# Four weights of a fused graph network rounded by ScalarE with their low parts on GpSimd, and two row splits moved behind the first group's last scaling

## The reference

```python
def reference(x, adj, nodemask, ...):
    x = _layernorm(x + _L0_gnn_ref(x, nodemask, adj, adj, W_qkv, W_out, b_out))   # attention
    x = _layernorm(x + _L1_gnn_ref(x, adj, W))                                    # mean aggregation
    x = _layernorm(x + _L2_gnn_ref(x, adj, W1, b1, gamma, beta, W2, b2))          # hypergraph
    x = _layernorm(x + _L3_gnn_ref(x, adj, Wqk, bqk, Wl, bl, Wr, Wd, bd))         # gated similarity
    return x

# L0: 8 heads of 64: attn = 0.33 * softmax(q k^T / 8, masked) + 0.33 * adj + 0.33 * exp(-adj)
#     out = (attn v) @ W_out + b_out
# L1: relu([x, (adj x) / max(deg, eps)] @ W^T)
# L2: h = relu(G (x W1^T) + b1); h = layer_norm(h) * gamma + beta; y = G (h W2^T) + b2; y + x
#     G = D^-1 H B^-1 H^T, H = (adj != 0), D weighted with adj's first row
# L3: xg = x * sigmoid(deg * Wd + bd); QK = sigmoid(xg Wqk^T + bqk); S = QK QK^T / 16 * adj
#     relu((S / rowsum) xg Wl^T + bl + xg Wr^T)
```

## Time and profile before

| | us |
|---|---|
| three timed runs, median (lowest, highest) | 1227.41 (1226.9, 1227.48) |
| the profiled execution, its time | 1225.61 |
| its span, first to last instruction | 1223.7 |
| TensorE busy (share of the span) | 1168.5 (95%) |
| VectorE busy | 896.1 (73%) |
| ScalarE busy | 586.5 (48%) |
| GpSimd busy | 583.7 (48%) |
| TensorE's granted clock, mean share of full speed | 0.981 |

### The profile page before, as it was taken

The page is one execution under the profiler, slowest core; times in us unless marked ns, Lnnn a source line. Parts: engine busy times, 40 slices in busy tenths (PEclk is TensorE's granted clock), DMA queues, the critical chain, the costliest instruction groups (busy, mean ns, idle before and its releaser), DMA issues.

```text
span 1223.7 us, 30667 instructions
## 1 busy us (share of the span) xinstructions
PE 1168.5 (95%) x11472; PEld 1037.0 (85%) x11472; DVE 896.1 (73%) x1983; ACT 586.5 (48%) x1186; POOL 583.7 (48%) x747
## 2 busy tenths in 40 slices
PE   5789999999999999999999999999999999999866
PEld 4678898988989898898989889898988989898755
DVE  3775777777777777777777777777777777778753
ACT  3336454454545445454544545454454545445231
POOL 2416447272644727264472726447272644727150
PEclk9799999999999999999999999999999999999897
DMA  7000002010010201001020100102010010100000
GB/s 221 23 27 23 23 2 66 2 45 21 15 49 0 64 0 43 21 14 51 0 64 0 43 21 13 51 0 64 0 43 21 12 52 0 47 2 27 1 22 18
DMA packets 52726, 37.12 MB, mean 30 GB/s; under 512 B 28166, under 2 KB 47564, under 8 KB 52684
## 3 DMA queue, kind: packets, MB, share of 16 engines
q1 hardware_dynamic: 51816, 36.14, 9.8%
q10 hardware_dynamic: 868, 0.40, 0.2%
HBM read 28.14 MB, written 8.39 MB: 30 GB/s over the span
## 4 chain that ended last, share of the span: by engine, by line
PE 91%; DVE 4%; POOL 2%; ACT 1%; issue 1%; DMA 1%; POOLq 0%; SPq 0%; DVEq 0%
PE bank L981 21%; PE bank L983 20%; PE bank L982 20%; PE bank L1177 7%; PE bank L1085 3%; PE bank L1052 3%; PE bank L1121 2%; PE bank L1063 2%; PE bank L1246 2%; PE bank L1229 2%; PE bank L1042 1%; PE bank L1150 1%; PE bank L1093 1%; PE bank L1219 1%; PE bank L1166 1%
## 5 line engine op out<-in xcount | busy, mean ns | idle before, releaser
L462 POOL TENSOR_SCALAR var<-mv 128x2 f32<-128x2 f32 x128 | 29.2, 228 | 381.3 <-DVE mv L764 381.2
L588 ACT ACTIVATE v<-bank 64x256 f32<-64x256 f32 x256 | 96.8, 378 | 77.5 <-PE bank L983 74.8
L771 DVE TENSOR_SCALAR x<-x,mv,rstd 128x256 f32<-128x256 f32 x256 | 120.2, 516 | 12.0 <-POOL rstd L465 12.0
L760 DVE BATCH_NORM_STATS2 stats<-x 128x6 f32<-128x256 f32 x256 | 96.4, 419 | 4.4
L465 POOL TENSOR_TENSOR rstd<-var,negh 128x2 f32<-128x2 f32 x128 | 91.0, 711 | 10.7
L887 DVE TENSOR_TENSOR hT_lo<-r,hT_hi 128x512 fp32r<-128x512 f32 x64 | 68.7, 1108 | 33.8 <-ACT hT_hi L616 33.8
L534 POOL TENSOR_TENSOR prob<-prob,mix 128x512 f32<-128x512 f32 x64 | 87.8, 1373 | 6.0 <-POOL prob L529 1.9
L529 POOL TENSOR_TENSOR prob<-prob,srec 128x512 f32<-128x512 f32 x64 | 70.8, 1107 | 40.0 <-DVE srec L812 40.0
L576 ACT ACTIVATE pT<-bank 128x512 f32<-128x512 f32 x64 | 34.5, 589 | 98.7 <-PE bank L1063 98.7
L694 DVE TENSOR_TENSOR spT_lo<-bank,spT_hi 128x512 fp32r<-128x512 f32 x64 | 44.2, 691 | 51.1 <-ACT spT_hi L576 51.1
L981 PE MATMUL bank<-wo_hi,oT_hi 128*128 128x256 f32 x256 | 76.0, 297 | 3.6 <-DVE oT_lo L694 3.4
(11 more groups left out here) (213 smaller groups left out, 3908.4 us busy)
## 6 DMA issues: line engine op xcount, KB each, us to landing
xTin<-in_x_t SPq DMA_DIRECT2D x32, 256.0 KB, 2.9
xin<-in_x SPq DMA_DIRECT2D x16, 512.0 KB, 3.7
out_x<-x SPq DMA_DIRECT2D x32, 256.0 KB, 2.2
adjA<-in_adj SPq DMA_DIRECT2D x16, 128.0 KB, 2.6
adjB<-in_adj SPq DMA_DIRECT2D x32, 64.0 KB, 3.2
adjC<-in_adj SPq DMA_DIRECT2D x32, 64.0 KB, 2.3
r<-in_wqkv SPq DMA_DIRECT2D x2, 512.0 KB, 8.5
x<-in_wqkv SPq DMA_DIRECT2D x1, 512.0 KB, 10.5
```

The costliest lines, as they stand in the source:

```text
L588: ins = act.activation(v[e * N:(e + 1) * N, i, gr, :, :], src[gr * N:(gr + 1) * N, e], ACT.Copy)
L760: dve.bn_stats(stats[layer][:, t, :], src[:, t, :]).then_inc(SEM[f"stats{n}"], 1)
L771: ins = dve.tensor_scalar(x[:, t, :], x[:, t, :], mv[layer][:, t, 0:1], rstd[layer][:, t:t + 1], ALU.subtract, ALU.mult)
```

## The change

Four of the five weights of group 0 (w1, wm, wqk and W2) are no longer split by VectorE. ScalarE rounds w1, wm and wqk behind its step `pv` 0 and W2 behind its `pv` 3; each counts the new semaphore `rounded`. GpSimd subtracts: the low parts of w1, wm and wqk behind its `soft` 3, that of W2 behind the reciprocal root of `norm0` 1; each counts `others_ready`. VectorE's `other_weights(0)` keeps only the two scalings of W2, `other_weights(1)` goes away, `other_weights(2)` keeps `tbc`, the correction and the two extra columns. The six instructions on adjacency's first row and the six on the bias row move to the end of `other_weights(3)`. Waits follow: VectorE's `norm0` 0 waits for w1's low part (its buffer is overwritten), ScalarE's `graph_a` for three low parts, TensorE's `mean` for two and `up` for four.

```diff
@@ -272,6 +272,9 @@
         w2_scaled = ctx.enter_context(nc.semaphore("w2_scaled"))
         ones_ready = ctx.enter_context(nc.semaphore("ones_ready"))
         weights_ready = ctx.enter_context(nc.semaphore("weights_ready"))
+        rounded = ctx.enter_context(nc.semaphore("weights_rounded"))
+        w2_fixed = ctx.enter_context(nc.semaphore("w2_fixed"))
+        others_ready = ctx.enter_context(nc.semaphore("other_weights_ready"))
         early_in = ctx.enter_context(nc.semaphore("early_in"))
         zero_ready = ctx.enter_context(nc.semaphore("zero_ready"))
         parted = ctx.enter_context(nc.semaphore("parted"))
@@ -489,6 +492,13 @@
                     pool.wait_ge(*count("sqsum", g, i - 1))
                 pool.tensor_tensor(r[:, 0, :], r[:, 0, :], r[:, i, :], ALU.add).then_inc(SEM["sqsum"], 1)
 
+            def norm0(g, i):
+                inv_root(g, 0, "0", 2 * i, 2 * i + 2, i)
+                if isinstance(g, int) and g == 0 and i == 1:
+                    pool.wait_ge(rounded, 4)
+                    pool.tensor_tensor(w2[1][:, :, 0:D], raw_2, w2[0][:, :, 0:D].bitcast(F32),
+                                       ALU.subtract).then_inc(others_ready, 1)
+
             def mean_h(g, i):
 
                 pool.wait_ge(*count("msq_ready", g, 1))
@@ -533,10 +543,15 @@
                 t = k - k % 2
                 pool.tensor_tensor(u, u, mix[:, t:t + 2, :].rearrange("p t (a n) -> p t a n", a=1)
                                    .broadcast_to([P, 2, HP, N]), ALU.add).then_inc(SEM["attn_ready"], 1)
+                if isinstance(g, int) and g == 0 and k == T - 1:
+                    for n, (pair, src) in enumerate(((w1, raw_1), (wm, raw_m), (wqk, raw_qk))):
+                        pool.wait_ge(rounded, n + 1)
+                        pool.tensor_tensor(pair[1][:, :, :], src, pair[0][:, :, :].bitcast(F32),
+                                           ALU.subtract).then_inc(others_ready, 1)
 
             steps = {
                 "soft": soft, "mask": residual,
-                "norm0": lambda g, i: inv_root(g, 0, "0", 2 * i, 2 * i + 2, i),
+                "norm0": norm0,
                 "graph_a": graph_a, "graph_b": graph_b, "gate": gate_argument, "split_low": split_low,
                 "mean": lambda g, i: inv_root(g, 1, "1", 2 * i, 2 * i + 2, i),
                 "hyper": lambda g, i: inv_root(g, 2, "2", 2 * i, 2 * i + 2, i),
@@ -598,9 +613,18 @@
                 src = bank_of("oT", i)
                 ins = act.activation(oT[0][:, i % 2:HP:2, :], src[:, :].rearrange("p (a n) -> p a n", a=HP // 2), ACT.Copy)
                 ins.then_inc(SEM["oT_hi"], 1)
+                if isinstance(g, int) and g == 0 and i == 0:
+                    act.wait_ge(weights_in, 16 * 8)
+                    for pair, src in ((w1, raw_1), (wm, raw_m), (wqk, raw_qk)):
+                        act.activation(pair[0][:, :, :], src, ACT.Copy).then_inc(rounded, 1)
+                if isinstance(g, int) and g == 0 and i == T - 1:
+                    act.wait_ge(w2_fixed, 1)
+                    act.activation(w2[0][:, :, 0:D], raw_2, ACT.Copy).then_inc(rounded, 1)
 
             def graph_a(g, i):
                 act.wait_ge(*filled("ht", 0, g))
+                if isinstance(g, int) and g == 0:
+                    act.wait_ge(others_ready, 3)
                 src = bank_of("ht", 0)
                 act.activation(flat(hTb[:, :, :]), src[:, 0:T * P // 2].bitcast(BF16), ACT.Copy)
                 ins = act.activation(flat(hT0[:, :, :]), src[:, 0:T * P // 2].bitcast(BF16), ACT.Copy)
@@ -712,7 +736,6 @@
 
                 if i == 0:
                     dve.wait_ge(weights_in, 16 * 8)
-                    split_weight(w1, raw_1)
                     dve.wait_ge(bias_in, 16 * 8)
                     for c in range(HC):
                         dve.tensor_scalar(xl[2][:, c, :], raw_2[:, c, :], bet[:, c:c + 1], None,
@@ -722,16 +745,7 @@
                     for c in range(HC):
                         dve.tensor_scalar(raw_2[:, c, :], raw_2[:, c, :], gam[:, c:c + 1], None,
                                           ALU.mult).then_inc(w2_scaled, 1)
-                    dve.wait_ge(zero_ready, 6)
-                    bias_parts(b2row, 0, 2 * D)
-                if i == 1:
-                    split_weight(wm, raw_m)
-                    split_weight(wqk, raw_qk)
                 if i == 2:
-
-                    three_parts([row0p[:, :, k] for k in range(3)], row0, gmat[:, 0, 0:T * GRP],
-                                gT[:, 0, 0:T * GRP])
-
                     dve.wait_ge(t_full, 1)
                     dve.tensor_copy(tbc[:, :], bank[7][:, 0:D]).then_inc(setup_dve, 1)
                     done[0] += 1
@@ -741,17 +755,21 @@
                     ones = one[:, :].rearrange("p (a k) -> p a k", a=1).broadcast_to([P, HC, 2])
                     setup(dve.tensor_copy(w2[0][:, :, D:D + 2], ones))
                     setup(dve.tensor_tensor(w2[1][:, :, D:D + 2], ones, ones, ALU.subtract))
-                    split_weight([half[:, :, 0:D] for half in w2], raw_2)
+                    dve.sem_inc(w2_fixed, 1)
                 if i == 3:
 
                     setup(dve.tensor_scalar(raw_lr, raw_lr, 0.5, None, ALU.mult))
                     setup(dve.tensor_scalar(bqk[:, :], bqk[:, :], 0.5, None, ALU.mult))
                     split_weight(wlr, raw_lr)
+                    three_parts([row0p[:, :, k] for k in range(3)], row0, gT[:, 0, 0:T * GRP],
+                                gT[:, 0, T * GRP:2 * T * GRP])
+                    dve.wait_ge(zero_ready, 6)
+                    bias_parts(b2row, 0, 2 * D)
 
             def pv(g, i):
                 low_part(g, "oT", i, oT[1][:, i % 2:HP:2, :], oT[0][:, i % 2:HP:2, :], "oT")
-                if isinstance(g, int) and g == 0 and i < 2:
-                    other_weights(i)
+                if isinstance(g, int) and g == 0 and i == 0:
+                    other_weights(0)
 
             def norm(g, layer, src, lo, hi):
 
@@ -816,6 +834,8 @@
                 dve.wait_ge(*filled("out0", i, g))
                 src = bank_of("out0", i)
                 dve.wait_ge(*count("xb_ready", g, 1))
+                if isinstance(g, int) and g == 0 and i == 0:
+                    dve.wait_ge(others_ready, 1)
                 ins = dve.tensor_tensor(flat(xl[0][:, lo:hi, :]), src[:, :], flat(xin[:, lo:hi, :]), ALU.add)
                 ins.then_inc(SEM["sum0_ready"], 1)
                 dve.wait_ge(*count("sum0_ready", g, i + 1))
@@ -1184,7 +1204,7 @@
 
             def mean(g, i):
                 if isinstance(g, int) and g == 0 and i == 0:
-                    pe.wait_ge(weights_ready, 6)
+                    pe.wait_ge(others_ready, 2)
                 pe.wait_ge(*count("turn1_lo", g, 2))
                 pe.wait_ge(*emptied("mean", i, g))
                 two_tiles("mean", i, lambda t: [(tile_of(x1T, c, t), chunk(wm, c)) for c in range(C)]
@@ -1198,7 +1218,8 @@
             def up(g, i):
                 if isinstance(g, int) and g == 0 and i == 0:
 
-                    pe.wait_ge(weights_ready, 9)
+                    pe.wait_ge(others_ready, 4)
+                    pe.wait_ge(weights_ready, 5)
                 pe.wait_ge(*emptied("up", i, g))
                 dst = bank_of("up", i)
                 now_full(product(dst[:, :], [(chunk(w1, c, slice(i * P, (i + 1) * P)), chunk(spT, c)) for c in range(C)],
```

## The result

The changed kernel takes 1233.74 us, median of 4 runs (1233.39 to 1235.09), the kernel before 1227.16 beside it (4 runs, 1224.25 to 1227.48). The ratio is 1.0061, 95% interval 1.0044 to 1.0078: slower by 0.4 to 0.8%. The profiled execution took 1235.09, with a span of 1233.3; it is the longest of the four.

What follows compares the result with a forecast made beforehand. TensorE, busy 95% of the span, was taken as the bound; +3.7 - 4.5 + 6.9 + 1.0 = +7.1 us on the profiled 1225.6 gave 1232.7, and the median's 1.8 more made 1234.5. The range was 1227.5 to 1238.

Steps and rivals of the forecast that it cites:

- `w2_sums` starts later: TensorE's start of `w2_sums`, held by VectorE's W2 scalings waiting on GpSimd's instructions: +3.7 us.
- `w2_sums` itself: Length of `w2_sums` on TensorE, left at 4.77 us, half at the low clock; bounds 3.14 and 6.40.
- second gap closes: TensorE's 3.43 us wait before `out0` 1 goes and it runs at full clock: -4.5 us, bounds -3.1 and -4.9.
- idle time before `graph_a`: TensorE waits for VectorE's longer chain to `edge`: 7.2 less 0.33 makes +6.9 us, bounds 4.4 and 7.2.
- low clock around `agg`: Low TensorE clock behind the new idle time before `graph_a`: +1.0 us, between 0 and 1.9.
- One scaling a turn: VectorE's eight W2 scalings pass singly between GpSimd's instructions, the last three after wqk, ending near 55.4 us.
- The rival of one run: VectorE and GpSimd, 45 to 49 us: all eight scalings pass together before 48.7; total -1.3, 1226.1 us; chance 0.13.
- the rival of two a turn: Two scalings pass between GpSimd instructions, the eighth ending near 52.2 us; `w2_sums` +0.6, total +4.0, 1231.4; chance 0.15.
- first rival: Not slower: VectorE's eight scalings pass in one run, `w2_sums` follows without a gap; 1226.1 us; chance 0.13.
- third rival: Low clock lasts longer: all of `w2_sums` low, +1.6, and +0.9 before `agg`; total +9.6, 1237.0 us; chance 0.15.
- the 0.33 in hand: Slack between VectorE finishing `edge` at 79.65 and TensorE taking it up at 79.98: 0.33 us.
- fourth rival: W2's low part on GpSimd does not delay `scale0` 1's scalings: -2.5, so total +4.6, 1232.0 us; chance 0.07.

Runs made afterwards that it cites:

- The filled gap: The changed kernel with 24 matmuls, their result overwritten, ahead of TensorE's wait for the scalings before `w2_sums`: 1233.65 us, ratio 1.0057 to the kernel before.
- the run with W2's low part later: The changed kernel with W2's subtraction on GpSimd moved from behind `norm0` 1 to behind `graph_b` of group 0: 1230.38 us, ratio 1.0034 to the kernel before.
- the subtractions that wait: The changed kernel with GpSimd's three subtractions behind `soft` 3 waiting until the eight W2 scalings are done: 1225.98 us, ratio 0.9998 to the kernel before.
- the second with filler: Repeat of the changed kernel with 24 overwritten matmuls ahead of the wait before `w2_sums`, beside the changed kernel: 1231.75 us, ratio 1.0045 to the kernel before.
- the row splits alone: The kernel before with only the bias and adjacency row splits moved behind `scale0` 1, all weights left with VectorE: 1229.03 us, ratio 1.0024 to the kernel before.

## Why the prediction was right, and where it was off

It said 1234.5, in a range of 1227.5 to 1238.0; 1233.74 came. The mechanism and the places were right; two terms were mis-sized, and part of the closeness is luck: errors that cancel.

| term | predicted | measured |
|---|---|---|
| `w2_sums` starts later | +3.7 | +3.46 |
| `w2_sums` itself | 0 | +1.49 |
| second gap closes | -4.5 | -4.53 |
| idle time before `graph_a` | +6.9 | +6.15 |
| low clock around `agg` | +1.0 | +2.28, then -1.67 |
| sum | +7.1 | +7.18 |

The first line holds the 0.17 by which the changed trace was late from the start.

- *One scaling a turn.* As said: one behind `soft` 2's end, one behind each of the next four instructions, three when wqk is done. They end at 55.01, not 55.4, since subtractions of 1024 elements take 2.40 and 2.38 and not the 2.49 of two halves. The working had a slip here: an end at 55.4 against 51.55 is +3.85, not the +3.7 that it took. The rival of one run needed an end before 49, the rival of two a turn one near 52.2; neither came. By the rule of the Trainium skill, "SBUF — State Buffer", section "Who interferes with whom", the sum was this one, and the trace agrees, with 2.43 and 2.31 for a scaling that needs 0.26 alone. The prediction put plain sharing of bandwidth with its first rival; but engines that share would end the scalings near 50 (an estimate: 2.3 us of scalings, from 1.14 for four, at half speed from 45.4), a case that got no price of its own. The ends one by one, each behind a GpSimd end, and GpSimd's 1.09 and 1.29 beside them speak against it.
- *The length of `w2_sums`.* The step that left it at 4.77 failed. The third rival had it at the low level throughout, +1.6 in all; +1.49 came. The filled gap shows that this is the clock and not the data's lateness.
- *The second gap.* -4.53 against -4.5: `out0` 1 has 0.41 of wait left and runs at full level.
- *Before `graph_a`.* The chain from VectorE's add to `edge` grew from 6.47 to 12.89, by 6.42; less the 0.33 in hand that makes 6.1. The row splits were right to the hundredth, 4.74. W2's subtraction was put at 2.49 and cost the scalings 1.88, because it takes 2.20 and began at 75.94, a little ahead of them. The two sum to 6.62, 0.20 over the 6.42: VectorE had a short pause ahead of `edge` in the kernel before (1.33 from the start of wlr's subtraction to the next instruction, 1.14 in the changed kernel), so it had some 0.5 in hand there and not 0.33. That W2's subtraction is in the way at all, against the fourth rival, the run with W2's low part later shows.
- *The clock behind it.* `agg` came 2.28 later than `graph_a`'s shift says, beyond the bound of 1.9; and the later stretch at half clock near 99 us (the window of before, above) went away, which nothing in the prediction had. Net +0.6 against +1.0, and that is luck: of the eleven profiles four have the low stretch (before, the subtractions that wait, W2's later low part, the second with filler) and seven do not, among them the row splits alone, where no weight has moved. What decides it is open. With it the shift would have been some 1.6 larger.
- *The range.* The upper end by the bounds of the clock terms, +1.6 and +0.9, is 1237.0 and not the 1236.5 that the working gives.

## What to carry to other kernels

Before work moves to GpSimd, ask what VectorE has queued in the same microseconds: many short VectorE instructions on SBUF tiles beside long GpSimd ones passed one a turn here, so either let GpSimd wait until they are through or make them few and wide. Moving setup work off a place where TensorE waits only helps if the place it goes to has slack; some 0.5 us was not enough for 6.6, while behind the gamma scalings the same row splits held up nothing. And count a wait of TensorE with the clock behind it: the same 16 matmuls took 3.34, 4.77 or 6.26 us.

## What the runs showed of the hardware

- The clock behind a wait does not follow from the wait's length alone. Behind 1.03, 1.19, 1.50 and 1.58 us `w2_sums` ran at 1.00, behind 2.16 and 3.00 half of it or somewhat more and behind 6.53 and 6.50 nearly all of it ran low; but behind the same 1.11 and 0.56 before aggregation's second call the clock fell to 0.50 in the kernel before and stayed at 1.00 in the changed one, and behind 6.07 in W2's later low part only the first half of `w2_sums` ran low.
- Not every VectorE instruction takes turns with GpSimd. In the changed kernel `oT_lo`, which reads one operand from a bank of PSUM, where TensorE leaves its products, and one from SBUF, the memory of the tiles, took 0.69 at 44.77 while GpSimd's L544 ran from 44.66 to 45.94, and 0.68 at 54.93 with GpSimd idle; the scalings and subtractions with all operands in SBUF were held.
- The start of round 1's work moves by -1.2 to +1.7 us from one execution to another, and a clock that rises sooner can move it further (-2.0 at the scalings of the run whose subtractions wait, whose transposes near 38 us took 1.09 in place of 1.97). So starts in two traces are compared only after a common instruction close ahead.
